# Attention and mixture kernel on one core: PSUM banks in rotation, expert tables before the first projections, and two recurrences added up by TensorE

## The reference, cut to what matters

```python
# cond: two linear recurrences over time per channel, forwards and backwards
decay = exp(-exp(w)) * (0.5 + 0.5 * tf)            # one number per channel and batch
nf, df = scan(a = a * decay + ek * f), scan(b = b * decay + ek)     # nb, db: the same in reverse
num = nf + nb - ek * f + euk * f
den = df + db - ek + euk
base = sigmoid(r) * (num / maximum(den, 1e-8)) * (0.8 + 0.2 * tf)   # r = x

x = x + attention(cond(x, f, f))        # 16 heads, 4 key heads, head size 128, q and k normed, causal
x = x + ffn(cond2(x, f, f))             # router, top 8 of 64 in 8 groups, group tables of 176 rows
```

## Time and profile before

| what | value |
| --- | --- |
| time, median of 3 runs | 416.05 us (415.28 to 416.07) |
| the profiled execution: its own time | 415.59 us |
| its span, first to last instruction | 413.8 us |
| granted TensorE clock, mean | 1.00 |
| busy PE, DVE, ACT, POOL | 89%, 79%, 67%, 53% |

### The profile page before, as it was taken

One profiled execution on the slowest core, in us unless ns is written; L12 is line 12 of the kernel. 1 busy time (PEld: TensorE's weight loads), 2 busy tenths in 40 slices (PEclk: granted clock), 3 DMA queues, 4 the chain that ended last, 5 costly groups with the idle time before them and its releaser, 6 DMA issues.

```text
span 413.8 us, 6407 instructions
## 1 busy us (share of the span) xinstructions
PE 367.6 (89%) x1952; PEld 295.0 (71%) x1952; DVE 326.0 (79%) x759; ACT 275.6 (67%) x673; POOL 218.7 (53%) x230
## 2 busy tenths in 40 slices
PE   0098869899999799898999997999899999999996
PEld 0097656688878667687787776687687878788884
DVE  8999789988988997599999889476567777665543
ACT  5547789798789497796978879784274434453321
POOL 7260614278524868134693121563269756888832
PEclk9999999999999999999999999999999999999999
DMA  6825300112100304001031000110065433365121
GB/s 207 308 76 197 104 0 3 49 57 99 52 0 2 103 0 154 1 2 51 2 101 40 1 2 0 38 48 32 2 186 160 140 115 97 96 216 166 53 76 51
DMA packets 14209, 31.92 MB, mean 77 GB/s; under 512 B 1872, under 2 KB 4432, under 8 KB 14176
## 3 DMA queue, kind: packets, MB, share of 16 engines
q1 hardware_dynamic: 13888, 31.38, 23.2%
q10 hardware_dynamic: 288, 0.14, 0.1%
HBM read 30.43 MB, written 1.08 MB: 76 GB/s over the span
## 4 chain that ended last, share of the span: by engine, by line
PE 66%; DVE 19%; ACT 11%; issue 3%; DVEq 0%; ACTq 0%
PE ov L1223 7%; PE sc L1201 7%; PE tr L1152 5%; PE proj L1140 4%; PE acc L1126 3%; PE acc L1128 3%; PE acc L1127 3%; PE proj L1144 3%; PE proj L1141 3%; PE acc L1317 2%; PE acc L1318 2%; PE tr L1127 2%; PE acc L1321 2%; PE tr L1126 2%; PE tr L1128 2%
## 5 line engine op out<-in xcount | busy, mean ns | idle before, releaser
L598 POOL TENSOR_TENSOR WL<-stage,WH 128x256 fp32r<-128x256 f32 x142 | 125.6, 913 | 75.6 <-ACT WH L664 75.6
L612 POOL TENSOR_TENSOR PR<-PR,RI 128x512 f32<-128x512 f32 x48 | 53.7, 1134 | 80.7 <-DVE RI L1072 80.7
L1140 PE MATMUL proj<-WH,RH 128*128 128x512 f32 x96 | 42.5, 442 | 32.0 <-DVE RL L923 19.9
L625 ACT ACTIVATE PR<-PR,MX 128x128 f32<-128x128 f32 (+1 forms) x128 | 56.6, 455 | 0.0
L1201 PEld LDWEIGHTS sc<-kT,QT 128*128 128x128 f32 x256 | 41.0, 191 | 15.8 <-issue 12.8
L1223 PE MATMUL ov<-PTS,V 128*128 128x512 f32 x96 | 46.6, 594 | 1.1 <-DVE OL L1084 1.1
L1201 PE MATMUL sc<-kT,QT 128*128 128x128 f32 (+1 forms) x256 | 47.2, 327 | 0.0
L1140 PEld LDWEIGHTS proj<-WH,RH 128*128 128x128 f32 x96 | 18.4, 192 | 38.6 <-issue 36.3
L1062 DVE CUSTOM_DVE_ANT_0 PR<-sc,const,RQ 128x128 f32<-128x128 f32 (+1 forms) x128 | 45.5, 411 | 0.1
L824 ACT CAST OH<-PR 128x512 fp32r<-128x512 f32 x22 | 13.6, 620 | 41.7 <-DVE PR L1108 41.7
L618 POOL TENSOR_TENSOR OL<-PR,OH 128x512 fp32r<-128x512 f32 x22 | 28.9, 1315 | 22.3 <-ACT OH L824 20.8
(11 more groups left out here) (166 smaller groups left out, 948.4 us busy)
## 6 DMA issues: line engine op xcount, KB each, us to landing
stage<-in_ffn SPq DMA_DIRECT2D x22, 384.0 KB, 3.3
stage<-in_wq SPq DMA_DIRECT2D x8, 512.0 KB, 3.3
stage<-in_wo SPq DMA_DIRECT2D x8, 512.0 KB, 3.3
SBC<-group_scalars SPq DMA_DIRECT2D x8, 256.0 KB, 3.6
PR<-in_tables SPq DMA_DIRECT2D x4, 352.0 KB, 7.4
fT<-in_fT SPq DMA_DIRECT2D x4, 256.0 KB, 4.0
xT<-in_xT SPq DMA_DIRECT2D x4, 256.0 KB, 4.5
stage<-in_wk SPq DMA_DIRECT2D x2, 512.0 KB, 4.9
```

The source lines that it names most:

```text
L598: i = pool.tensor_tensor(lo[:, c:c + 256], src[:, c:c + 256], hi[:, c:c + 256].bitcast(F32), ALU.subtract)
L612: pool.tensor_tensor(pr, pr, RI[:, m % 4, hs[0]:hs[0] + nh].rearrange("p (h o) -> p h o", o=1).broadcast_to([P, nh, 512 // nh]), ALU.mult) ...
L625: return nc.scalar.activation(o, i, ACT.Exp, **k)
L1140: mm(proj[:], rh[ch], wh[ch], start=ch == 0, stop=False, skip_group_check=True)
```

## The change

**PSUM.** `proj`, `tr0`, `tr1` and `ov` become four banks `shared0` to `shared3`. Every projection, transpose and routing product takes the next of `shared0` to `shared2` in TensorE's order, and waits for the eviction of the step that held this bank last (three such steps back); E keeps `shared3`. From the first FFN step on, two of them rotate and the other two are the up banks.

**Opening.** TensorE starts with R 0 to 6, and the first key projection comes after them; all eight tables are loaded straight to buffers that are not in use yet, first in the queue. The R steps' masks are written by one GpSimd copy in place of eight. A projection waits for the low part only ahead of the matmuls that read it.

**Recurrences.** For layer 1 of batches 0 and 1, TensorE adds up df + db + the bonus term and nf + nb + the bonus term, as float32 matmuls with the identity into `sc0` and `sc1` (steps `sum`), and VectorE reads the sums from PSUM (12 counted instructions). In all of layer 1 the gate is now 1 + exp(-x) (ScalarE an exponential, GpSimd a capped addition), multiplied into the denominator together with the maximum; there is one activation table load where there were two.

**Tables.** `table` is two ScalarE copies of all rows, and the rest GpSimd's in place of VectorE's.

**Places.** `START`, `ORDERS` and the lists of iterations are new.

```diff
 START = {
-    "PE": [("split", "K", 0), ("small",), ("split", "Q", 0), ("K1", 0, 0), ("R", 0), ("K1", 0, 1), ("R", 1),
-           ("R", 2), ("R", 3), ("R", 4), ("R", 5), ("K3", 0, 0), ("K3", 0, 1)],
+    "PE": [("R", 0), ("R", 1), ("sum", 0, 0), ("R", 2), ("sum", 0, 1), ("sum", 0, 2), ("R", 3),
+           ("R", 4), ("R", 5), ("R", 6), ("K1", 0, 0), ("R", 7), ("split", "K", 0), ("small",),
+           ("split", "Q", 0), ("K1", 0, 1), ("sum", 1, 0), ("sum", 1, 1), ("K3", 0, 0), ("K3", 0, 1), ("sum", 1, 2)],
...
+def bank_plan():
...
+        if st[0] in POOLED or st[0] == "route" and st[2] not in (2, 5):
+            k = OUT_BANK if st[0] == "E" else n % (2 if late else OUT_BANK)
+            bank[st], old[st] = k, holder.get(k)
+            holder[k] = st
+            n += st[0] != "E"
...
             side(0)
+            sp.dma_start(mup[:], ins["mup"]).then_inc(s["mup_in"], 16)
+            table(0)
             sp.dma_start(const[:], ins["const"]).then_inc(s["consts_in"], 16)
-            main(0)
-            sp.dma_start(mup[:], ins["mup"]).then_inc(s["mup_in"], 16)
+            table(1)
+            table(2)
+            load(0)
+            table(3)
+            table(4)
+            side(1)
+            table(5)
+            load(1)
+            load(2)
+            table(6)
+            table(7)
             main(1)
             main(2)
             main(3)
-            load(0)
-            side(1)
-            table(0)
-            table(1)
-            table(2)
-            load(1)
-            table(3)
-            load(2)
-            table(4)
-            table(5)
...
+                elif st[0] == "ex":
+                    b = st[1]
+                    pool.wait_ge(s["gate_exp"], b + 1)
+                    pool.tensor_scalar(gate1(b), gate1(b), GATE_CAP, 1.0, ALU.min, ALU.add).then_inc(s["gate_ready"], 1)
+                elif st[0] == "table":
...
+                    linked(pool.tensor_scalar(SX[:, 0, part], SX[:, 0, part].bitcast(F32), table_rest, None, ALU.mult))
+                    for g in range(4 * h, 4 * h + 4):
...
+                        i = pool.tensor_tensor(EX[rows, h, :, table_col(g):table_col(g) + FI], hi, x, ALU.add)
...
                 elif k == 5:
...
+                    if summed(L, b):
+                        dve.wait_ge(s["sum_ready"], 2 * SUMMED.index(b) + 1)
+                        dve.wait_ge(s["gate_ready"], b + 1)
+                        done(v.scalar_tensor_tensor(out=DF, in0=sum_bank(b, 0), scalar=1e-8, in1=gate1(b), op0=ALU.max, op1=ALU.mult))
+                        return
...
-                        done(v.scalar_tensor_tensor(out=NF, in0=gate1(b), scalar=1.0, in1=NF, op0=ALU.add, op1=ALU.mult))
...
-                elif st[0] == "table":
...
-                        i = v.scalar_tensor_tensor(out=ex, in0=ex.bitcast(F32), scalar=table_rest[rows, :],
...
             def project(st, p, t, wst):
...
-                wait_proj_free(pe, st)
+                wait_evicted(pe, BANK_OLD[st])
+                proj = bank_of(st)
...
+                elif st[0] == "sum":
+                    _, b, k = st
+                    n0 = wkv_before(ND, 1, b)
+                    if k == 1:
+                        pe.wait_ge(s["wkv_dve"], n0 + 8)
+                    for x, n, kind in ((DF, 3, 0), (DB, 4, 0), (EUX[:], 5, 0), (NF, 6, 1), (NB, 7, 1), (EU[:], 9, 2)):
+                        if kind == k:
+                            pe.wait_ge(s["wkv_dve"], n0 + n)
+                            i = mm(sum_bank(b, min(k, 1)), ident, x, start=n in (3, 6), stop=n in (5, 9), skip_group_check=True)
```

More of the change, by code:

```diff
@@ L60 @@
     "ACT": ["GT", "split", "last", "GH"],
-    "DVE": ["GU", "last", "out"],
-    "POOL": ["split", "GL"],
+    "DVE": ["GU", "out", "last"],
+    "POOL": ["GL", "split"],
 }
@@ L97 @@
            "route": (0, 1, 3, 4, 6, 7, 8)},
-    "ACT": {"split": None, "small": None, "K1": None, "V": None, "K2": None, "K3": None, "table": None,
+    "ACT": {"ex": None, "split": None, "small": None, "K1": None, "V": None, "K2": None, "K3": None, "table": None,
             "wkv": (1, 6, 7), "gate": (0, 1), "route": (0, 2, 3, 5, 6, 7, 8)},
-    "DVE": {"K1": None, "K2": None, "table": None, "onehot": None, "wkv": (0, 2, 3, 4, 5, 6, 8), "gate": (0, 1),
+    "DVE": {"K1": None, "K2": None, "onehot": None, "wkv": (0, 2, 3, 4, 5, 6, 7, 8), "gate": (0, 1),
@@ L101 @@
             "route": (1, 2, 4, 5, 6, 7)},
-    "POOL": {"split": None, "small": None, "zeros": None},
+    "POOL": {"ex": None, "table": None, "split": None, "small": None, "zeros": None},
 }
@@ L153, in make_plan @@
     ahead = []
-    for f, places in enumerate(([36, 37, 37], [45, 45, 45])):
+    for f, places in enumerate(([36, 39, 39], [45, 45, 45])):
         for kind, i in zip(("GA", "GB"), places):
@@ L218 @@
 PLAN = PLANS["PE"]
-BLOCKS = [s for s in PLAN if s[0] in ("small", "split") or s[0] == "R" and s[1] >= 6]
+BLOCKS = [s for s in PLAN if s[0] in ("small", "split")]
 BLOCK_NO = {s: n for n, s in enumerate(BLOCKS)}
```

317 lines of the change are left out of this document (177 added, 140 removed), and 12 rows, old and new, of the table ORDERS.

## The result

The changed kernel takes **410.6 us** (409.84 to 411.44, 4 runs) against 415.69 us (415.28 to 416.07, 4 runs) of the kernel before beside it. The ratio is 0.9878, 95% interval [0.9851, 0.9906]: faster by 5.1 us. The forecast was 405.3 us, 10.8 us less than before: the value lies inside its range, and less than half of the forecast gain is there. The profiled execution took 410.0 us with a span of 408.2.

The account below looks back on a forecast made before the run. TensorE was taken as the bound, busy 367.6 of 413.8 us; the span less 2.6 (opening) and 8.1 (banks) gave 403.1, plus 1.8 and 0.46 made 405.3 us, range 399 to 412.

Parts of the forecast that it names:

- the banks' term: Projections' waits for the one bank, 12.1 us: rotation removes their reason; two thirds taken, -8.1 us, bounds nothing and 12.1.
- the table work on GpSimd: Recurrence tables moved from VectorE to GpSimd: costed at nothing, bounds nothing and 5.7 us a half.
- The opening with the sums: Batches 0 and 1 before the first query projection: earlier start 1.3 us plus R 7's 1.36, together -2.6 us.
- Each time: Opening: first matmul near 6.7, batch 0's end 19, key projection 23.3, first squares 28.9, query projection 34.5.
- The second term: R 7 at 37.28 costs PE 1.36 us now; with all R steps done earlier, that was counted as gain.
- as "right" was defined: Sign in the changed trace: waits of projections for squares and values under 2 us together.
- the sign for "wrong": Sign in the changed trace: the same microseconds of waiting at scores, transposes and E.
- waits only move: Rival: bank waits become waits for maxima or low parts; 410.5 us (408.5 to 414); 0.24, shared with the last rival.
- the rival of the slow opening: Opening at half pace: first query projection 10.2 us later; 416.8, up to 421 us; slower had 0.07.
- up to 4.5 us given back: VectorE beside GpSimd: ten table operations at 0.45 us each would give back 4.5 of the 4.7 us relief.
- The row of the prediction: A VectorE scan took 1.23 us at 6.30 and 1.68 at 24.53, beside GpSimd's subtractions.
- Places, 0: New step places, touching the same idleness plus 9 us more: taken at 0, between -4 and +4 us.

Follow-up runs that it names:

- the old places: Changed kernel with the step order and places of the kernel before behind the opening: 416.17 us, ratio 1.0018.
- the subtractions cut: Changed kernel with GpSimd's weight subtractions cut to 32 of 1024 columns: 403.03 us, ratio 0.9696.
- the rotation alone: Kernel before with only the banks changed, projections and transposes rotating over three: 411.38 us; with subtractions cut to 32 of 1024 columns 402.23 us.
- light tables: Changed kernel, GpSimd's table work cut to one addition of 32 partitions and a 32-column scaling for each half: 407.22 us, ratio 0.9813.
- the filler: Changed kernel with VectorE's eviction D1 moved ahead, plus four float32 identity matmuls ahead of item 3's transposes: 408.66 us, ratio 0.9839.
- the one swapped pair: Changed kernel with VectorE's eviction D1 listed ahead of two background steps, which swaps one pair near 192: 409.26 us, ratio 0.9858.

## Why the prediction was wrong, point by point

Two terms of the sum failed. The larger is the size of the banks' term: 8.1 us forecast, 4.1 measured. The other is the table work on GpSimd: nothing forecast, about 3.4 us measured. The opening with the sums gave about 1.3 more than its 2.6, and the places 0.3, so 4.0 + 3.4 - 1.3 - 0.3 = 5.8, against the 5.7 us by which the gain of 5.1 falls short of 10.8. The opening's 3.9 is what the other steps leave over, not a run of its own.

**The opening: right in its places, wrong in its price.** Each time was met within 0.6 us, but for VectorE's squares (0.8 us early) and the tables' arrival (8.24 instead of 6.7). R 0 and R 1 made up for most of that: they took 3.95 us together, not 5.1. I priced the opening at 1.3 + 1.36. The second term was no gain, since something else hid behind it. R 7 stood at 37.28 behind a query projection, while ScalarE copied that projection's result for the next transposes. The copy ended at 38.07 and the transposes started at 38.48, so R 7 cost at most 0.4 us. Now TensorE waits at the same place for 1.58 us for this copy. What arrived at the transposes is 0.98 us, as the text itself had it ("about 1.0 us earlier"), before it carried on 1.3 and added 1.36.

**"POOL is idle for 66%", so "I cost it at nothing": failed.** Measured: about 3.4 us, 5.0 in the old places, between the bounds of nothing and 5.7 a half. The 66% and the 80.7 us of waiting for divisions are an average; I did not ask where in the queue the second half stands. It stands ahead of two splits and item 3's division. I named only the value weights' split as the one who waits. Of item 3's wait 1.4 us and the fall of the clock behind it (1.7 us) went with the table work; the other 2.4 us belong to the splits, and with the subtractions cut no wait for a division is listed any more.

**Banks, -8.1: the mechanism is right, the size fails.** The 12.1 us fell to 1.6, as "right" was defined, but the sign for "wrong" was there too: 8.5 of them came back at other instructions with the rotation alone, most at transposes. Alone it gave 4.1, and 8.9 with GpSimd's subtractions out of the way. I took two thirds from the idle time of VectorE and ScalarE. The text did say that transposes would wait for divisions, but GpSimd's work stood in no bound of this term. That 8.9 comes near 8.1 is luck in part, since that kernel was not the one forecast. The rival *waits only move* said that the waits would become ones for maxima and low parts; it had the size nearly (410.5 against 410.6) and the place wrong: they are for a division, for evictions and for the copies of queries.

**The clock was no term at all.** It was 1.00 everywhere in the profiled execution before (other executions of that kernel have means from 0.994 to 1.00, at no different time), and I used it only in the rival of the slow opening. In the changed kernel 3.4 us are lost to slow work behind waits of 3.80 and 2.16 us. The Trainium skill (TensorE: Matmul & The Clock Gate, "HAM oscillation — how this bites in real kernels") says that gaps in a kernel's matmul work throttle TensorE again, and that each gap is paid for once more in slow matmuls; the trace agrees where the gap of 3.8 us was filled, with 1.6 us given back, and not at every gap: full pace followed 2.14 us of waiting in the kernel before. What a fall costs the whole can be read from executions of one kernel. The old places take 414.36 to 416.13 us at a mean clock of 0.992 (five) and 416.15 to 417.62 at 0.988 (seven); the light tables 405.99 to 407.22 at 0.994 or 0.995 (three) and 408.81 and 409.49 at 0.990.

**VectorE beside GpSimd, "up to 4.5 us given back".** The Trainium skill (SBUF — State Buffer, "SBUF: two separate sides") has the two engines exclude each other for the whole instruction, when VectorE reads two inputs from SBUF or works in one of its two-port modes. The trace now agrees better than it did: two-input operations of 0.68 us take 1.4 beside GpSimd's table additions of 1.0 us each, and one of a single input 1.05 in place of 0.43. In which mode that one works no run shows. The row of the prediction had shown 0.45 us for a scan. What this traffic and GpSimd's queue cost together is 4.3 us before and 7.6 after; these runs do not part the two.

**Places, 0:** 0.3 alone. Within the bounds of 4 there, not with the new opening and tables (5.6).

The sum as measured, in steps that runs stand at: 415.7, rotation 411.4, places 411.1, opening with sums and tables 410.6. The last step is 0.5: about 3.4 lost to the tables, so about 3.9 won by opening and sums, of which VectorE's relief is a part. Steps of 0.3 and 0.5 are smaller than what nearly equal kernels differ by here. Only 0.98 of it was seen as a head start.

## What to carry to other kernels

An engine's idle share says nothing about what a step moved to it costs. Walk its queue at the place where the step will stand, list what is behind it, and ask when TensorE needs that. Price a wait of TensorE twice: its length, and the slow stretch that may follow it; and where a stall that is removed was someone's cover, as the copy was for R 7, take that someone out of the gain. When a change is worth little, cut the suspected engine's work in the kernel before as well as in the kernel after: the difference of the two differences, here 4.1 against 8.9 us for the rotation, tells that the change works and what hides it.

## What the runs showed of the hardware

- TensorE's granted clock fell to its lower level behind single waits of 3.80, 3.03, 2.45, 2.43, 2.33, 2.16, 2.13, 2.10, 2.08 and 2.03 us in these kernels, and did not behind others of 2.44, 2.43, 2.40, 2.17, 2.16, 2.14, 2.07 and 2.03. So under 2.5 us the length of one wait does not tell. A fall cost 1.6 to 3.4 us. The same wait near 211 (2.07 to 2.16 us) was followed by a fall in the changed kernel, with light tables and with the filler, and not in the version with the one swapped pair, so a single execution tells little of it.
- GpSimd's time did not shrink with fewer partitions: an addition of 32x352 took 0.95 us (mean of 8), 2.7 ns a column, and a subtraction of 128x256 0.74 (median of 142), 2.9 ns a column. A scaling of 128x352 took 1.19 us, a division of 128x512 1.04 when alone. But a minimum-and-add with two constants on 128x512 took 1.94 to 2.36 us, about twice the two-input operation of the same shape.
- In the rotation alone VectorE's 759 instructions were busy for 326.9 us beside GpSimd's full subtractions and for 305.7 beside the cut ones.

```profile
L654 POOL TENSOR_TENSOR EX<-SX,SCRX 32x352 fp32r<-32x352 f32 x8 | 7.6, 945 | 0.6
L643 POOL TENSOR_SCALAR TH<-TH 128x512 f32<-128x512 f32 x2 | 4.4, 2212 | 1.1 <-ACT TH L684 1.1
```
